# Two-step attention kernel: fewer GpSimd instructions in the threshold guess, a ScalarE sum moved one slot later, and another end fraction in step two

## The reference

```
def _adj_from_feats(Xa, W1, W2, W3):
    logits = Q @ W2 @ K.T / TAU                 # 3327 x 3327
    vals = take_along_axis(logits, idx, axis=1) # each row sorted, largest first
    csum = cumsum(softmax(vals, axis=1), axis=1)
    k_i = sum(csum < P_NUC, axis=1) + 1         # P_NUC = 0.9
    ...                                         # keep the first k_i, softmax over them
for s in range(STEPS):                          # STEPS = 2
    A = _adj_from_feats(Xa, W1, W2, W3)
    Xf = Rf @ Xf; Xb = Rb @ Xb; Xa = A @ Xa
    Z = Z + (Xf @ U1[s] + Xb @ U2[s] + Xa @ U3[s])
```

## Time and profile before

| | before |
|---|---|
| time, median of 3 runs | 3471.04 us (3469.64 to 3474.25) |
| the profiled execution's own time | 3468.18 us |
| its span in the profile | 3466.4 us |
| PE busy | 3137.2 us (91%) |
| DVE busy | 2444.9 us (71%) |
| POOL busy | 2140.7 us (62%) |
| ACT busy | 1598.2 us (46%) |
| instructions on POOL | 4214 |

### The profile page before, as it was taken

One profiled execution on the slowest core, in us unless ns is written; L12 is line 12 of the kernel. 1 busy time (PEld: TensorE's weight loads), 2 busy tenths in 40 slices (PEclk: granted clock), 3 DMA queues, 4 the chain that ended last, 5 costly groups with the idle time before them and its releaser, 6 DMA issues. The chain is left out here.

```text
span 3466.4 us, 42065 instructions
## 1 busy us (share of the span) xinstructions
PE 3137.2 (91%) x13212; PEld 2267.5 (65%) x13212; DVE 2444.9 (71%) x3401; ACT 1598.2 (46%) x2357; POOL 2140.7 (62%) x4214
## 2 busy tenths in 40 slices
PE   4999999997899999999966698988999999996899
PEld 3888778885567777777754255544566566664788
DVE  6840123333998889888884799999988999998000
ACT  2311322225666666666753455655555555552200
POOL 2212422224788888888880677877888788786211
PEclk9999999998899999999988899999999999998899
DMA  7644344433112222222211111211222222223255
GB/s 258 239 146 146 116 156 166 165 129 87 44 54 59 60 64 58 59 60 64 58 33 63 47 57 48 63 44 55 58 82 75 73 85 82 74 83 103 92 202 173
DMA packets 140702, 327.59 MB, mean 95 GB/s; under 512 B 15456, under 2 KB 93664, under 8 KB 129248
## 3 DMA queue, kind: packets, MB, share of 16 engines
q1 hardware_dynamic: 140512, 325.30, 29.5%
HBM read 286.70 MB, written 38.54 MB: 94 GB/s over the span
## 5 line engine op out<-in xcount | busy, mean ns | idle before, releaser
L1030 ACT ACTIVATE junk<-E,negp 128x3327 uint8<-128x3327 f32 x208 | 637.3, 3064 | 142.8 <-issue 112.0
L1401 DVE SCALAR_TENSOR_TENSOR U<-E,trial 128x3327 f32<-128x3327 f32 x182 | 674.7, 3707 | 0.0
L925 PE MATMUL bank<-big,adj 128*128 128x512 f32 x1352 | 611.4, 603 | 11.2 <-ACT t L1056 11.2
L925 PEld LDWEIGHTS bank<-big,adj 128*128 128x128 f32 x1352 | 253.5, 193 | 333.3 <-issue 332.2
L298 PE MATMUL bank<-big,E 128*128 128x256 f32 x1664 | 364.7, 381 | 1.9 <-PEq L58 1.7
L885 PE MATMUL bank<-Hc,PT 128*128 128x256 f32 x1248 | 303.2, 395 | 66.7 <-ACT PT L1069 66.4
L298 PEld LDWEIGHTS bank<-big,E 128*128 128x128 f32 x1664 | 315.0, 191 | 48.3 <-issue 5.4
L885 PE MATMUL bank<-Hc,adj 128*128 128x256 f32 x1456 | 336.3, 383 | 9.4 <-ACT adj L1069 9.4
L1363 DVE TENSOR_REDUCE nmax<-E 128x1 f32<-128x3327 f32 x52 | 187.9, 3614 | 206.2 <-ACT E L1073 206.2
L885 PEld LDWEIGHTS bank<-Hc,PT 128*128 128x128 f32 x1248 | 244.7, 198 | 127.3 <-ACT PT L1069 77.9
L885 PEld LDWEIGHTS bank<-Hc,adj 128*128 128x128 f32 x1456 | 278.3, 192 | 72.1 <-issue 22.5
(11 more groups left out here) (248 smaller groups left out, 5729.7 us busy)
## 6 DMA issues: line engine op xcount, KB each, us to landing
adj<-adjT SPq DMA_DIRECT2D x131, 448.0 KB, 3.4
E<-adjT SPq DMA_DIRECT2D x32, 1664.0 KB, 6.9
adj<-adjT SPq DMA_DIRECT2D x104, 384.0 KB, 3.3
adj<-adjT SPq DMA_DIRECT2D x20, 1664.0 KB, 6.9
E<-adjT SPq DMA_DIRECT2D x26, 1216.0 KB, 5.7
xt<-xin SPq DMA_DIRECT2D x52, 128.0 KB, 5.6
xt<-x_d SPq DMA_DIRECT2D x52, 128.0 KB, 5.3
xo_d<-xo SPq DMA_DIRECT2D x26, 256.0 KB, 3.7
```

Source lines behind the costliest of these rows:

```text
L925: last = mm(agg[:, 0:w], adj[:, SPAN * (k % 2) + j - AGG[k]], rhs[:, j], start=(j == 0), stop=False)
L1030: go(junk[:, 0:N], E[:, t % DEPTH, 0:N], func, bias=negp[:, t % 2, j:j + 1], scale=1.0, accum_out=acc_[:, t % 2, j:j + 1]).then_inc(summed ...
L1401: V_.scalar_tensor_tensor(out=U[:, 0:N], in0=e, scalar=point, in1=e, op0=ALU.is_ge, op1=ALU.mult, accum_out=found))
```

## The change

It has three parts. (1) POOL's guess and corrections are written with fewer instructions: a shift is folded into another instruction, three scalings of the row sum become one instruction over three columns, and `up[3]`, `up[4]` are no longer worked out at the end of the guess, where nothing read them. (2) For the second point, the first of ACT's two sums moves from slot 0 to slot 1 of the round for all of step one but its last tile. (3) `KEEP_END` of step two goes from 0.75 to 0.85.

```diff
-KEEP_END = (0.8, 0.75)
+KEEP_END = (0.8, 0.85)
...
-                                if k == 0 and R is not None:
+                                if k == 0 and R is not None and R >= NT - 1:
                                     sums(R, 1, 0)
...
+                                    if R is not None and R < NT - 1:
+                                        sums(R, 1, 0)
                                     if R is not None:
                                         sums(R, 1, 1)
...
-                        def prepare(t):
-                            q, step = t % 2, t // NT
-                            p = cand[:, q, 0:1]
-                            then(ts(up[:, q, 0:2], known[:, 4 + 2 * step:6 + 2 * step], p, ga[:, q, 12:13], ALU.mult, ALU.add),
-                                 ts(up[:, q, 3:4], p, p, RIDGE[step] ** 2, ALU.mult, ALU.mult))
-                            then(tt(up[:, q, 4:5], up[:, q, 3:4], ga[:, q, 11:12], ALU.mult))
+                        def aims(t):
+                            q, step = t % 2, t // NT
+                            return ts(up[:, q, 0:2], known[:, 4 + 2 * step:6 + 2 * step], cand[:, q, 0:1],
+                                      trial2[:, t % DEPTH, NEG:NEG + 1], ALU.mult, ALU.add)
...
-                            then(ts(ga_(7), ga_(6), 2.0, 0.01, ALU.mult, ALU.add),
-                                 ts(ga_(8), ga_(5), 1.0, -SHIFT[step], ALU.mult, ALU.add))
+                            then(ts(ga_(7), ga_(6), 2.0, 0.01, ALU.mult, ALU.add))
                             then(tt(ga_(9), ga_(7), half, ALU.pow),
-                                 tt(ga_(10), ga_(8), ga_(7), ALU.add))
+                                 ts(ga_(10), ga_(7), -SHIFT[step], ga_(5), ALU.add, ALU.add))
...
                             then(tt(shape4(parts[:, 0]), z.to_broadcast([P, 4]), shape4(outset[:, 0]), ALU.mult),
-                                 ts(tgt, z, P_NUC, None, ALU.mult),
-                                 ts(ga_(12), z, -P_NUC, None, ALU.mult),
+                                 tt(trial2[:, d, GOAL:NEG + 1:2], z.to_broadcast([P, 3]), known[:, 8:11], ALU.mult),
                                  tt(ga_(15), z, minus, ALU.pow))
                             then(tt(ends2[:, d], parts[:, 0], outset[:, 1], ALU.add),
-                                 ts(below, tgt, 1 - 2.0 ** -24, None, ALU.mult),
+                                 aims(t),
                                  ts(ga_(11), ga_(15), ga_(9), 1.0 / DENSITY, ALU.mult, ALU.mult))
-                            prepare(t)
...
                             if j < POINTS - 1:
-                                then(ts(p, up_(23), hi, lo, ALU.min, ALU.max))
-                                offer(t, j + 1)
-                                prepare(t)
+                                then(ts(negp[:, q, j + 1:j + 2], up_(23), lo, -UNDER, ALU.max, ALU.mult),
+                                     ts(p, up_(23), lo, None, ALU.max))
+                                pool.sem_inc(aimed[j + 1], 1)
+                                then(aims(t), ts(up_(3), p, p, RIDGE[step] ** 2, ALU.mult, ALU.mult))
+                                then(tt(up_(4), up_(3), slope, ALU.mult))
```

More of the change, by code:

```diff
@@ L44 @@
 SPAN = 7
-POINT, GAP, GOAL, MASS, BELOW = 0, 1, 2, 3, 4
+POINT, GAP, GOAL, MASS, BELOW, NEG = 0, 1, 2, 3, 4, 6
 @contextmanager
@@ L1253, in update @@
                             then(ts(mass_, count, p, over[:, q, j:j + 1], ALU.mult, ALU.add))
-                            then(ts(cand[:, q, 1:3], up[:, q, 0:2], mass_, None, ALU.add),
-                                 ts(took[:, 1:2], mass_, tgt, None, ALU.is_ge))
-                            if j > 0:
-                                then(tt(up_(16), mass_, up_(7 + j), ALU.subtract))
+                            if j == 0:
+                                then(ts(cand[:, q, 1:3], up[:, q, 0:2], mass_, None, ALU.add),
+                                     ts(took[:, 1:2], mass_, tgt, None, ALU.is_ge),
+                                     ts(took[:, 0:3:2], mass_.to_broadcast([P, 2]), tgt, None, ALU.is_lt))
+                                then(ts(up_(21), slip, slope, STRIDE, ALU.mult, ALU.min))
+                            else:
+                                then(ts(cand[:, q, 1:3], up[:, q, 0:2], mass_, None, ALU.add),
+                                     tt(up_(16), up_(7 + j), mass_, ALU.subtract),
+                                     ts(took[:, 1:2], mass_, tgt, None, ALU.is_ge),
+                                     ts(took[:, 0:3:2], mass_.to_broadcast([P, 2]), tgt, None, ALU.is_lt))
@@ L1258, in update @@
                                 then(ts(up_(17), up_(16), up_(16), up_(3), ALU.mult, ALU.add),
-                                     tt(up_(18), up_(16), up_(20), ALU.mult))
+                                     ts(up_(18), up_(16), up_(20), up_(4), ALU.mult, ALU.add))
                                 then(tt(up_(19), up_(17), minus, ALU.pow),
-                                     tt(up_(18), up_(4), up_(18), ALU.subtract))
-                                then(tt(slope, up_(18), up_(19), ALU.mult))
@@ L1263, in update @@
-                            then(tt(up_(21), slip, slope, ALU.mult),
-                                 ts(took[:, 0:3:2], took[:, 1:2].to_broadcast([P, 2]), -1.0, 1.0, ALU.mult, ALU.add))
+                                     tt(up_(22), up_(18), slip, ALU.mult))
+                                then(ts(up_(21), up_(22), up_(19), STRIDE, ALU.mult, ALU.min))
                             wide = lambda ap: ap.unsqueeze(2).to_broadcast([P, 2, 2])
-                            then(ts(up_(20), up_(21), STRIDE, -STRIDE, ALU.min, ALU.max),
+                            then(ts(up_(20), up_(21), -STRIDE, None, ALU.max),
@@ L1271, in update @@
                                  tt(ends, parts[:, 0], parts[:, 1], ALU.add))
[L1272 removed]
+                            then(ts(up_(23), up_(22), p, hi, ALU.mult, ALU.min))
                             if j < POINTS - 1:
[L1274 to L1276 removed]
+                                then(ts(negp[:, q, j + 1:j + 2], up_(23), lo, -UNDER, ALU.max, ALU.mult),
[3 more added lines that the diff above has]
+                                then(tt(up_(4), up_(3), slope, ALU.mult))
                             else:
[L1278 removed]
+                                then(ts(point, up_(23), lo, None, ALU.max))
                                 pool.sem_inc(bracketed, 1)
```

16 lines of the change are left out of this document (6 added, 10 removed).

## The result

| | before | changed |
|---|---|---|
| median, on the same chip | 3471.36 us (4 runs) | 3454.26 us (3453.95 to 3454.52, 4 runs) |
| ratio | | 0.9949, 95% interval 0.9937 to 0.9961 |
| span of the profiled execution | 3466.4 us | 3452.6 us |
| instructions on POOL | 4214 | 3905 |

What follows compares the result with a forecast made beforehand. POOL, slowed by DVE's passes, was taken to bound step one at 38.9 us a round. The terms 28 + 3 + 9 - 1 = 39 us off 3468.2 gave 3429 us, 3432 on the runs' scale, range 3410 to 3452 us.

Steps and rivals of the forecast that it cites:

- What bounds the kernel: Layer 2: POOL bounds step one at 38.9 us a round, DVE step two's first half, PE its second half.
- Part 1, the guess: POOL's guess in step one: 1.4 us less per tile, 28 us over 20 rounds and 3 us in three more.
- Part 1, the corrections: POOL's two corrections: counted at nothing, with bounds of 0.5 us either way per tile.
- The stalls' rival: Step one: POOL waits off its gain at DVE's next pass, rounds stay at 38.9 us; 3462 us, chance 13%.
- Part 2, the move: ACT's sum in step one: PE no longer idles for slot 1's copies; costed at nothing beyond part 1.
- The slower rival: Step one: two sums back to back hold slot 2's copies and PE waits for them; 3522 us, chance 4%.
- Part 3, the end fraction: Step two's search: 72 passes for 74; tile 27 gives 8.9 us, tiles 44 and 47 nothing, tile 50 costs 1 us.
- The signs I named: L1030's wait in slot 1, L1069 waits under 12 us, 20 rounds in 745 to 755 us, 72 passes, half of step two 9 us shorter.

Runs made afterwards that it cites:

- 2: Kernel before the change with only the first sum for the second point moved from slot 0 to slot 1: 3464.62 us, ratio 0.9978.
- 7: Changed kernel with the first correction in its old grouping; shorter guess, second correction, moved sum and end fraction stay: 3431.38 us, ratio 0.9881 to the kernel before.
- 10: Kernel of 7 with the second point's first sum put back into slot 0: 3443.18 us, ratio 0.9917 to the kernel before.
- 1: Changed kernel with the moved sum put back into slot 0, the rest of the change kept: 3488.66 us, ratio 1.0045 to the kernel before.
- 12: Kernel of 7 with the release of the second point in step one moved behind POOL's next group: 3438.37 us, ratio 0.9904 to the kernel before.
- number 3: Kernel before the change with only the end fraction of step two set to 0.85: 3462.62 us, ratio 0.9977, 72 passes.
- number 5: Changed kernel with one small chained DVE instruction (0.2 us) a tile ahead of the masking pass in step one: 3448.0 us, ratio 0.993 to the kernel before.
- number 9: Kernel of 7 with one small POOL instruction (0.2 us) a tile ahead of the clamp in step one: 3451.11 us, ratio 0.9936 to the kernel before.

## Why the prediction was wrong, point by point

**What bounds the kernel.** Right for the changed kernel's step one, where POOL's chain through DVE's passes closes the round (it goes with the guess); right for step two, with DVE as the bound of the first half and PE of the second, which did not move. For the kernel before I had one of two paths: "POOL's chain is closed without it", I said of the moved sum, but DVE's last wait there was for ACT's scores 16 times and for POOL's release twice, and the sum in slot 0 lay on that path (2).

**Part 1, the guess.** The total was right: with the old first correction the 20 rounds give 771.3 - 744.2 = 27.1 us against the forecast 28, tiles 23 to 25 give 2.2 us against 3. Partly luck, as this includes the move and the shorter second correction, which I had at nothing. With the sum in slot 1 in both, POOL's part gives 767.8 - 744.2 = 23.6 us (2 and 7), 1.2 us a steady round where I had 1.4; with the sum in slot 0 in both, 771.3 - 754.8 = 16.5 us (before and 10).

**Part 1, the corrections: the step that failed.** "In the two corrections I count nothing", with 0.5 us either way per tile. The first correction costs 0.7 us a steady round: the guess ends at S + 25.6 in place of S + 24.9 us, and 755.2 - 744.2 = 11.0 us of the 20 rounds go there. At the same place the release slips from S + 15.6 to S + 19.4 us, which I had not priced at all: with the first correction's share it makes 5.1 us in tiles 23 to 25. All told, the regrouped first correction costs 22.8 us of the profiled span (3452.6 against 3429.8), and it accounts for what is missing: 3431.4 us with it undone, 3432 forecast. Of these 22.8 us, 6.7 lie elsewhere: 0.3 at the start, 2.1 at the turn to step two, -0.6 from there to tile 28, 3.6 in the rest of its first half and 1.3 at the end; the experiments do not take these apart. That 3431.4 and 3432 agree so well is luck in part: the terms don't agree as well.

The reason is that I added durations. From the second L1401 on the changed correction stands one group further back. At the third it is caught in `ends`, with the product `up[23]` still to come, where the old one is caught in that product. From the end of that pass to the start of L1408 there is 0.6 us, room for one link and a bit. The old correction uses it for the clamp and slips `negp` in; the changed one uses it for the product, and `negp` and `p` are left to do behind the pass. An instruction that is caught costs nothing more than the pass, so what each kernel pays is what it has left then.

**The stalls' rival** had part of the mechanism, and 13%. It said that the gain would be waited off at the next pass; in truth the guess kept its gain and the correction lost some. My counterargument, that DVE's passes "move along" with the round, doesn't hold for the first correction: L1408 begins 15.2 us behind S and the correction 4.5 us behind S in the changed kernel as in number 7, whatever the guess has gained.

**Part 2, the move.** Right in that PE then waits for slot 2's copy; "I cost it at nothing beyond part 1" was wrong, because in slot 0 the sum lengthens the path through ACT's scores, which was the last one in the kernel before. It gives 7 us by itself (0.9978), 12 us with the old first correction (7 against 10), and 34 us in the changed kernel (1), where slot 0 can't bear the late release. So the moved sum and the regrouped correction hide each other: in slot 1 the late release costs 7 us (12 against 7), in slot 0 it turns the gain into a loss. The slower rival's mechanism, slot 2's copies coming late, shows as 21.1 us in 16 waits of PE against 3.1 us in 6 in number 7. It isn't what lengthens the round: number 12 has 11.1 us of such waits and the round of number 7.

**Part 3, the end fraction.** Right: 72 passes, in the tiles named. Tile 27's gave 8.0 us (7.5 alone) against 8.9; from PE's start on tile 37 to the end, where tile 50's is, the changed kernel takes 0.6 us more than before and number 3 takes 1.3 more, with 1 charged.

**The signs I named.** L1030's wait moved to slot 1 and 72 passes were there. The 20 rounds, by PE's starts, were to take 745 to 755 us and took 759.3 (743.5 in number 7), and PE's waits for L1069 were to be under 12 us and were 21.1. These two pointed at POOL's step. The first half of step two became 6.3 us shorter by PE's starts (549.5 to 543.2), with 9 forecast.

The Trainium skill says that GpSimd's SBUF interfaces are shared with VectorE, with contention when a VectorE instruction has two SBUF inputs (GPSIMD Engine Reference, Specifications). The traces agree: the masking pass has two, and an instruction of 0.3 us takes 3.76 us under it. I had drawn from it that 18.4 us a round are lost whatever POOL does. In the changed kernel's round above each of the five passes does catch one POOL instruction (L1334, L1251, L1269, L1272, L1247). But the sum does not say which instruction falls behind a pass, nor what is left behind it.

## What to carry to other kernels

Where short instructions of one engine are held up by long ones of another, don't sum durations: lay the two timelines side by side and count what is left to do when each long one ends, since 0.2 us can move a whole instruction across its start. Look at who is released there as well, and let the instruction that nobody waits for be the one that is caught. A time that comes out as expected is not yet the mechanism: number 5 hit its number with the release as late as before.

## What the runs showed of the hardware

- The edge is sharp, but it lies in another place for each form of instruction. A `negp` without a pointer operand that began 0.02 us after DVE's pass took 0.25 us; one with a pointer operand took 0.30 us when it began 0.10 us ahead of the pass (number 5) and 3.76 us when it began 0.09 us after it. The clamp with two pointer operands began 0.02 us ahead of a pass and took 3.77 us (number 9). The traces of all 14 kernels, taken together, say the same of starts near DVE's two-input passes: `negp` without a pointer operand got through up to 0.03 us behind the pass's start and was caught from 0.07 us behind it on; with one it got through when it began at least 0.10 us ahead, and was always caught from 0.01 us ahead on; the correction's second instruction (L1247 in the changed kernel), with two, got through up to 0.17 us ahead and was caught from there on. So of these three, the one with more pointer operands has to begin earlier. Why, no run here shows.
- More work for an engine that isn't the bound made the kernel faster: 3446.6 us with three more instructions a tile on DVE, 3454.3 without.
